# Image tokenizer's synthesis split by column bands, GpSimd's rotation in three functions, and new written orders of a step for all engines

## What is computed

```python
def reference(x, cls_tok, ...):
    h = tok(x)            # rec = idwt2(rec, h * w[0], v * w[1], d * w[2]), level by level
    h = concatenate([cls_tok, h], axis=1)
    h = h + attn(layernorm(h))
    h = h + ffn(layernorm(h))
```

## Time and profile before

| | |
|---|---|
| median of 3 runs | 1755.23 us (1753.16 to 1758.5) |
| span of the profiled execution | 1750.5 us, first to last instruction; no other time of that execution is given |
| PE busy | 1664.2 us, 95% |
| DVE busy | 1470.0 us, 84% |
| ACT busy | 1323.6 us, 76% |
| POOL busy | 1120.1 us, 64% |

### The profile page before, as it was taken

One profiled execution on the slowest core, in us unless ns is written; L12 is line 12 of the kernel. 1 busy time (PEld: TensorE's weight loads), 2 busy tenths in 40 slices (PEclk: granted clock), 3 DMA queues, 4 the chain that ended last, 5 costly groups with the idle time before them and its releaser, 6 DMA issues.

```text
span 1750.5 us, 48653 instructions
## 1 busy us (share of the span) xinstructions
PE 1664.2 (95%) x16742; PEld 1278.3 (73%) x16742; DVE 1470.0 (84%) x4972; ACT 1323.6 (76%) x3812; POOL 1120.1 (64%) x1034
## 2 busy tenths in 40 slices
PE   7758999999999999999999999999999999999975
PEld 6635777777777777777777777777777777777653
DVE  3837888899888888899888888899888888889874
ACT  0326888888888888888888888888888888888762
POOL 0087667766777666766777667666677667666500
PEclk9789999999999999999999999999999999999986
DMA  9311111111111111111111111111111111111100
GB/s 320 110 61 61 56 53 56 53 67 57 61 68 68 59 61 57 50 65 62 56 68 68 66 55 60 54 56 66 55 64 68 68 53 61 56 53 62 44 7 13
DMA packets 90168, 113.70 MB, mean 65 GB/s; under 512 B 14818, under 2 KB 52163, under 8 KB 89667
## 3 DMA queue, kind: packets, MB, share of 16 engines
q1 hardware_dynamic: 89922, 110.59, 18.1%
HBM read 26.62 MB, written 8.42 MB: 20 GB/s over the span
## 4 chain that ended last, share of the span: by engine, by line
PE 88%; DVE 4%; SPq 3%; POOL 2%; ACT 1%; issue 1%; DMA 0%; DVEq 0%; POOLq 0%; ACTq 0%
PE bank L725 45%; PE bank L842 9%; PE bank L983 7%; PE bank L831 6%; PE bank L829 6%; PE bank L994 3%; PE bank L853 3%; PE bank L903 3%; PE bank L891 2%; PE bank L1003 2%; SPq L320 1%; PE bank L882 1%; DVE arena L1283 1%; PE bank L950 0%; POOL rot L486 0%
## 5 line engine op out<-in xcount | busy, mean ns | idle before, releaser
L482 POOL TENSOR_TENSOR arena<-rq,cos 128x512 f32<-128x512 f32 x256 | 326.1, 1274 | 280.0 <-ACT rq L526 280.0
L535 ACT ACTIVATE arena<-arena,nm 128x129 f32<-128x129 f32 (+1 forms) x1024 | 455.6, 455 | 0.0
L486 POOL TENSOR_TENSOR rot<-rot,sin 128x512 f32<-128x512 f32 x256 | 326.3, 1275 | 103.9 <-DMA rot<-rq 103.9
L725 PE MATMUL bank<-xt_h,weights 128*128 128x256 f16 x2048 | 378.9, 273 | 9.2 <-ACT rq L526 7.8
L526 ACT ACTIVATE rq<-bank,bqk 128x256 f32<-128x256 f32 x512 | 214.4, 471 | 170.1 <-PE bank L725 155.3
L1283 DVE CUSTOM_DVE_ANT_0 arena<-bank,bias 128x129 f32<-128x129 f32 (+1 forms) x1024 | 317.9, 352 | 26.5 <-issue 16.6
L489 POOL TENSOR_TENSOR arena<-arena,rot 128x512 f32<-128x512 f32 x256 | 314.2, 1228 | 37.3 <-POOL rot L486 0.9
L1291 DVE TENSOR_TENSOR ptr_l<-bank,ptr_h 128x384 f16<-128x384 f32 x512 | 280.0, 552 | 31.8 <-ACT ptr_h L545 29.4
L545 ACT ACTIVATE ptr_h<-bank 128x384 f16<-128x384 f32 x512 | 249.1, 486 | 68.6 <-PE bank L725 44.0
L725 PE MATMUL bank<-xt_l,weights 128*128 128x256 f16 x1024 | 279.6, 273 | 0.0
L842 PE MATMUL bank<-eye,arena 128*128 128x128 f32 x1536 | 253.0, 277 | 8.5 <-DVE ptr_l L1291 4.4
(11 more groups left out here) (200 smaller groups left out, 3182.5 us busy)
## 6 DMA issues: line engine op xcount, KB each, us to landing
rot<-rq SPq DMA_DIRECT2D x512, 128.0 KB, 2.0
arena<-in_x SPq DMA_DIRECT2D x4, 2048.0 KB, 15.2
xin<-in_x SPq DMA_DIRECT2D x32, 256.0 KB, 2.8
hr<-hr SPq DMA_DIRECT2D x32, 256.0 KB, 2.3
out<-h SPq DMA_DIRECT2D x64, 128.0 KB, 2.1
arena<-in_L_attn_w_qkv SPq DMA_DIRECT2D x2, 1536.0 KB, 8.6
weights<-in_L_ffn_w_down SPq DMA_DIRECT2D x1, 1024.0 KB, 11.8
arena<-in_L_ffn_w_gate SPq DMA_DIRECT2D x1, 1024.0 KB, 8.5
```

Of the source, the lines that this page charges most:

```text
L482: pool.tensor_tensor(dst, rq[:, g % 2].rearrange("p j (t n) -> p j t n", t=T), cos[:, :].rearrange("p (t n) -> p t n", t=T).unsqueeze(1).b ...
L486: pool.tensor_tensor(r, r, sin[:, :].unsqueeze(1).broadcast_to([P, 2, SIDE]), ALU.mult).then_inc(t2_ready, 1)
L535: act.activation(cols, cols, ACT.Exp, bias=nm[:, t, h:h + 1], scale=-1.0, accum_out=rs[:, t, h:h + 1]).then_inc(e_done, 1)
L725: ins = pe.matmul(dst, lhs[l], rhs[r], start=start and n == 0, stop=stop and n == len(parts) - 1)
```

## The change

It changes how tokens are made. POOL now takes sums and differences of neighbouring columns, level by level (`column_bands`), into a tile `haar` of 512 columns: 256, 128, 64 and 64 for the four column bands. `synthesise` multiplies each by its row operator, four matmuls of these widths into `b_bank`; `coarse` is gone. ACT copies the bank to `syn` (`synthesis_out`), and POOL undoes the column transform in six instructions (`image_back`) that write `hh`; DVE's `image_out` is gone. The gates' coefficients are set up for this in the first part, with four terms in place of three. `project(b, 5)` waits for ACT's copy in place of `hh`. `rotate` on POOL becomes `cosine`, `sine` and `turned_sum`, which stand apart in the order. Epsilon is added to the two variances by two instructions of one column each. Each engine's step has a new order, SP's too: there `store(s - 2, 1)` now stands ahead of `rotate(s, 0)`, and the load of an image waits for POOL's first column step, not for PE's product.

```diff
-BANDS, OPS, TERMS, BLOCK = 10, 4, 3, 8
+BANDS, OPS, TERMS, BLOCK = 10, 4, 4, 8
...
-                sp.wait_ge(syn_ready, a)
+                sp.wait_ge(coeffs, 3 * a - 2)
                 load_x(a)
...
             def step(s):
                 rotate(s - 1, 3)
                 rotate(s - 1, 4)
-                load(s + 1)
                 rotate(s - 1, 5)
+                rotate(s - 1, 7)
                 rotate(s - 1, 6)
-                rotate(s - 1, 7)
-                store(s - 3, 1)
+                move(s - 2)
+                store(s - 2, 0)
+                load(s + 2)
+                store(s - 2, 1)
                 rotate(s, 0)
                 rotate(s, 1)
                 rotate(s, 2)
-                move(s)
-                store(s - 2, 0)
...
+
+                pool.tensor_tensor(high, src[:, :, 0::2], src[:, :, 1::2], ALU.subtract)
+                return pool.tensor_tensor(low, src[:, :, 0::2], src[:, :, 1::2], ALU.add)
+
+            def column_bands(first):
+
+                d1, d2, d3, low = columns(haar)
+                column_step(s1[:, :, :], d1, xin).then_inc(coeffs, 1)
+                pool.wait_ge(coeffs, first)
+                column_step(s2[:, :, :], d2, s1).then_inc(coeffs, 1)
+                pool.wait_ge(coeffs, first + 1)
+                column_step(low, d3, s2)
+
             def first_operators():
 
...
-                pool.tensor_tensor(rowop[:, :, :].rearrange("p o (b r) -> p o b r", r=BLOCK),
-                                   ops[:, 0, :, :].unsqueeze(2).broadcast_to([P, OPS, P // BLOCK, BLOCK]),
-                                   avg[:, 2, :].rearrange("p (b r) -> p b r", r=BLOCK).unsqueeze(1).broadcast_to([P, OPS, P // BLOCK, BLOCK]), ALU.mult).then_inc(rowop_ready, 1)
+                build_rowop(ops[:, 0, :, :])
...
 
             def row_operators(a):
                 if not image(a) or a == 0:
                     return
                 pool.wait_ge(ops_ready, 2 if a <= 16 else 3)
                 pool.wait_ge(syn_ready, a)
-                pool.wait_ge(coarse_ready, a)
                 pool.tensor_copy(op_now[:, :, :], ops[:, bass.ds(a, 1), :, :].rearrange("p a o r -> p (a o) r")).then_inc(coeffs, 1)
                 pool.wait_ge(x_in, 16 * (a + 1))
-                pool.tensor_tensor(s1[:, :, :], xin[:, :, 0::2], xin[:, :, 1::2], ALU.add).then_inc(coeffs, 1)
-                pool.wait_ge(coeffs, 3 * a + 2)
-                pool.tensor_tensor(rowop[:, :, :].rearrange("p o (b r) -> p o b r", r=BLOCK),
-                                   op_now[:, :, :].unsqueeze(2).broadcast_to([P, OPS, P // BLOCK, BLOCK]),
-                                   avg[:, 2, :].rearrange("p (b r) -> p b r", r=BLOCK).unsqueeze(1).broadcast_to([P, OPS, P // BLOCK, BLOCK]), ALU.mult)
-                pool.tensor_tensor(s2[:, :, :], s1[:, :, 0::2], s1[:, :, 1::2], ALU.add).then_inc(coeffs, 1)
-                pool.wait_ge(coeffs, 3 * a + 3)
-                pool.tensor_tensor(s3[:, :, :], s2[:, :, 0::2], s2[:, :, 1::2], ALU.add).then_inc(rowop_ready, 1)
+                column_bands(3 * a + 1)
+                build_rowop(op_now[:, :, :])
+
+            def image_back(a):
+                if not image(a) or begun and a == 0:
+                    return
+                d1, d2, d3, low = columns(syn)
+                pool.wait_ge(syn_out_done, a + 1)
+                pool.tensor_tensor(quad_sum[:, :, 0::2], low, d3, ALU.add)
+                pool.tensor_tensor(quad_sum[:, :, 1::2], low, d3, ALU.subtract).then_inc(back, 1)
+                pool.wait_ge(back, 2 * a + 1)
+                pool.tensor_tensor(pair_sum[:, :, 0::2], quad_sum[:, :, :], d2, ALU.add)
+                pool.tensor_tensor(pair_sum[:, :, 1::2], quad_sum[:, :, :], d2, ALU.subtract).then_inc(back, 1)
+                pool.wait_ge(back, 2 * a + 2)
+                if a:
+                    pool.wait_ge(hr_ready, a)
+                    pool.wait_ge(xn_ready, a)
+                pool.tensor_tensor(hh[:, :, 0::2], pair_sum[:, :, :], d1, ALU.add)
+                pool.tensor_tensor(hh[:, :, 1::2], pair_sum[:, :, :], d1, ALU.subtract).then_inc(h_ready, 1)
...
-            def rotate(b, g):
+            def cosine(b, g):
                 if not image(b):
...
+                pool.tensor_tensor(rope_out(b % 2, GROUPS[g]), rq[:, g % 2].rearrange("p j (t n) -> p j t n", t=T),
                                    cos[:, :].rearrange("p (t n) -> p t n", t=T).unsqueeze(1).broadcast_to([P, 2, T, P]), ALU.mult).then_inc(pcos_done, 1)
+
+            def sine(b, g):
+                if not image(b):
+                    return
                 pool.wait_ge(rot_done[g % 2], 128 * b + 32 * (g // 2 + 1))
                 r = rot[:, g % 2]
                 pool.tensor_tensor(r, r, sin[:, :].unsqueeze(1).broadcast_to([P, 2, SIDE]), ALU.mult).then_inc(t2_ready, 1)
+
+            def turned_sum(b, g):
+                if not image(b):
+                    return
+                dst = rope_out(b % 2, GROUPS[g])
                 wait_cos(pool, b, g)
                 pool.wait_ge(t2_ready, 8 * b + g + 1)
-                pool.tensor_tensor(dst, dst, r.rearrange("p j (t n) -> p j t n", t=T), ALU.add).then_inc(qk_done, 1)
+                pool.tensor_tensor(dst, dst, rot[:, g % 2].rearrange("p j (t n) -> p j t n", t=T), ALU.add).then_inc(qk_done, 1)
 
...
             first_operators()
+            image_back(0)
+            begun = True
             pool.wait_ge(late_in, 16 * 13)
 
             def step(s):
-                rotate(s + 1, 0)
-                rotate(s + 1, 1)
-                rotate(s + 1, 2)
-                row_operators(s + 2)
+                cosine(s + 1, 0)
+                add_bias(s + 1)
+                sine(s + 1, 0)
+                cosine(s + 1, 1)
+                turned_sum(s + 1, 0)
+                sine(s + 1, 1)
+                cosine(s + 1, 2)
+                turned_sum(s + 1, 1)
                 token_rstd(s)
-                rotate(s + 1, 3)
-                rotate(s + 1, 4)
-                rotate(s + 1, 5)
+                sine(s + 1, 2)
+                cosine(s + 1, 3)
+                turned_sum(s + 1, 2)
+                sine(s + 1, 3)
+                image_back(s + 2)
+                turned_sum(s + 1, 3)
+                cosine(s + 1, 4)
                 image_rstd(s + 2)
-                rotate(s + 1, 6)
-                rotate(s + 1, 7)
-                add_bias(s + 2)
+                cosine(s + 1, 5)
+                sine(s + 1, 4)
+                sine(s + 1, 5)
+                turned_sum(s + 1, 4)
+                turned_sum(s + 1, 5)
+                cosine(s + 1, 6)
+                cosine(s + 1, 7)
+                sine(s + 1, 6)
+                row_operators(s + 3)
+                turned_sum(s + 1, 6)
+                sine(s + 1, 7)
+                turned_sum(s + 1, 7)
...
 
-            def coarse_out(a):
+            def synthesis_out(a):
                 if not image(a):
                     return
-                act.wait_ge(coarse_ready, a + 1)
+                act.wait_ge(syn_ready, a + 1)
                 if a:
                     act.wait_ge(h_ready, a)
-                act.activation(pair_sum[:, :, :].rearrange("p t n -> p (t n)"), u_bank[:, 0:SIDE], ACT.Copy).then_inc(coarse_out_done, 1)
+                act.activation(syn[:, :], b_bank[:, :], ACT.Copy).then_inc(syn_out_done, 1)
...
-                pe.matmul(b_bank[:, :], rowop[:, 0, :], xin[:, :, :].rearrange("p t n -> p (t n)"), start=True, stop=True).then_inc(syn_ready, 1)
-
-            def coarse(a):
...
-                    if o > 0:
-                        rhs = rhs.unsqueeze(2).broadcast_to([P, T * n, 128 // n])
-                    ins = pe.matmul(u_bank[:, 0:SIDE], rowop[:, o + 1, :], rhs, start=o == 0, stop=o == 2)
-                ins.then_inc(coarse_ready, 1)
+                for o, (dst, src) in enumerate(zip(columns(b_bank), columns(haar))):
+                    ins = pe.matmul(dst.rearrange("p t n -> p (t n)"), rowop[:, o, :], src.rearrange("p t n -> p (t n)"), start=True, stop=True)
+                ins.then_inc(syn_ready, 1)
 
             def project(b, g):
                 if not image(b) or begun and (b, g) == (0, 0):
@@ -911,7 +958,7 @@
                 if g == 0:
                     pe.wait_ge(xtl_done, b + 1)
                 elif g == BEFORE_SYN and image(b + 1):
-                    pe.wait_ge(h_ready, b + 2)
+                    pe.wait_ge(syn_out_done, b + 2)
                 else:
                     pe.wait_ge(rq_ready, 8 * b + g)
                 for i in range(2):
...
-                ts(shifted[:, :], agg[:, :, 1], 1e-5, None, ALU.add).then_inc(ready, 1)
+                for t in range(T):
+                    ins = ts(shifted[:, t:t + 1], agg[:, t, 1:2], 1e-5, None, ALU.add)
+                ins.then_inc(ready, 1)
...
-                if not image(a) or begun and a == 0:
-                    return
-                dve.wait_ge(syn_ready, a + 1)
-                dve.wait_ge(coarse_out_done, a + 1)
...
```

(24 more changed lines are left out.)

348 lines of the change are left out of this document (160 added, 188 removed).

## The result

The changed kernel takes 1806.67 us (median of 4 runs, 1805.67 to 1810.37), the kernel before 1754.66 beside it: a ratio of 1.0307, 95% interval 1.0289 to 1.0325. The forecast was 1754 us with a range of 1712 to 1770. It was wrong.

A forecast was written before the change was run, and what follows sets the result against it. PE was taken as the bound at 49.04 us per step; -1.3 of product and +1.6 of wait gave +9 us, the ends -8, so 1756 by the sum, stated as 1754 us, range 1712 to 1770.

The forecast's parts named there:

- The place and the mechanism of the wait: PE at project_v(s, 1) waits for DVE's values_lo(.., 0), delayed by normalise_image blocked by POOL: 1.6 us per step.
- The size of the block: DVE's two normalise_image instructions, held up by POOL's unbroken run: +1.3 us per step (0.9 to 1.6).
- PE's product: Synthesis on PE: 2.26 us go, 0.96 come, so PE's work falls 1.3 us per step (1.07 to 1.39).
- The step that failed: PE's step: nothing behind project_v(s, 1) makes its wait good, so 49.3 us per step, +9 us over 29 steps.
- rival 1: No wait on POOL, or DVE has time: step 47.7 plus 0 to 0.3, 1709 to 1718 us; 0.32 with halfway cases.
- Rival 2: SP's store ahead of rotate(s, 0) makes POOL's chain late and DVE wait at image_stats: 1783 us; chance 0.15.
- The first part: Start, images 0 and 1: PE's 6.54 us wait for s3 shrinks as row_operators(1) moves ahead; -8 us (-13 to -3).
- The end: Last 84 us, holding no synthesis, with the chain that of the last block: 0 us (-2 to +3).

The follow-up runs named there:

- e1: Changed kernel with normalise_image written as scalar_tensor_tensor, rstd broadcast along the row, instead of tensor_scalar, same place in every order; 1794.97 us.
- e6: Changed kernel with xn of images 1 to 31 as an accumulating tensor_scalar in the same place, leaving out the factor rstd; 1759.82 us.
- e10: Changed kernel with SP's store(s-2,1) moved behind rotate(s,2) instead of ahead of rotate(s,0); 1806.03 us.
- e8: Kernel before the change with normalise_image(s-1) moved ahead of reciprocals(s-3,2) on DVE; 1826.57 us.
- e9: e8 with xn of images 1 to 31 as an accumulating tensor_scalar, leaving out the factor rstd; 1782.19 us.
- e14: Changed kernel with accumulating xn (no rstd, images 1 to 31), DVE's image_stats behind gate_up(s-3,0), POOL's image_rstd behind sine(s+1,5); 1789.08 us.
- e15: Changed kernel with xn (images 1 to 31) on ACT behind values_hi(s+1,0), image_stats behind gate_up(s-3,0), image_rstd behind sine(s+1,5); 1771.69 us.

## Why the prediction was wrong, step by step

- **The place and the mechanism of the wait**: right. `project_v(s, 1)` waits for `values_lo(., 0)`, because the pair of `xn` now meets POOL's rotations. Forecast 1.6 us per step; the mean is 1.36. What the prediction takes from the Trainium skill (SBUF — State Buffer, Who interferes with whom) on the tensor_scalar agrees with the 2.24 us of the earlier trace rows and the 2.39 here. The same section says that an instruction with two inputs in SBUF contends with a GpSimd instruction that reads SBUF, and that the tensor_scalar that writes out an accumulator does not enter the modes that contend. The 1069 and the 474 ns of e1 and e6 agree with both.
- **The size of the block**: too small. "The second by a whole one, 1.27 less what it would overlap: +1.3 us (0.9 to 1.6)" is +1.74 in the mean (2.39 less 0.65), and +2.04 in the step shown. The two instructions were held up by 0.8 and 0.9 us in the mean, not by 0.6 and what is left of 1.27. This is 0.4 us per step in the mean.
- **That the wait came out near its forecast** is luck in part. In the step shown, DVE's stretch from the start of `residual` to the end of `values_lo(., 0)` is 22.2 us where the forecast has 21.2 (19.91 and 1.3), and PE's from the end of `attention_out` is 20.9 (22.58 less the 1.65 idle) where it has 19.9. Both are too short by 1.0, and the difference hides it.
- **PE's product**: 1.3 us forecast, bounds 1.07 to 1.39. By the starts, 2.26 less 1.05 is 1.21. Three of the four narrow passes take 0.11 us, as one of 128 columns does, and the first takes 0.06; the weight loads in front of them, of 128 columns, start 0.11 apart. The row of 64-column loads that I called nearest was not. The Trainium skill (TensorE: Matmul & The Clock Gate, LDWEIGHTS) gives a load as its columns divided by 1.2, in ns; the estimate from it for 128 columns, 107 ns, agrees with these 0.11. Worth 3 us in all.
- **The step that failed**: "the wait at `project_v(s, 1)` becomes 1.6 us. Nothing behind it makes it good [...]: 49.04 - 1.3 + 1.6 = 49.3 us per step." This sum holds only if PE waits nowhere else in the new order. It does, and for reasons that have nothing to do with the block: e6, with the block gone and no wait at `project_v(., 1)`, has a step of 49.41, where the prediction's rival 1 gave 47.7 to 48.0. 1.5 us per step went there: 0.39 at `gate_up(., 1)`, 0.30 at `values(., 15)`, and the rest in pieces of at most 0.2. I had followed DVE against PE to one meeting point and taken the rest of a wholly new list to be as tight as the old one.
- **Rival 1** (no block, 1709 to 1718): wrong by the same 1.5 us. Without the block it would have been 1760. So the saving of PE's product would have been lost anyway.
- **Rival 2** (SP's store makes POOL late, 1783): not so. e10 moves the store and the time stays.
- **The first part**: -8 forecast; from the product of image 0 to that of image 2 it is -3.0. PE's two waits for `s3` there, 10.9 us with the 6.54 of the earlier trace rows, are gone. But its waits for ACT's `rq` grew from 8.9 to 14.5 us, those for `xn` from 2.3 to 4.0, and one of 2.9 for DVE's `gs` is new. The longest of those for `rq` in the changed kernel:

```profile
108.33 0.28 PE L783 MATMUL bank<-xt_h,weights 128*128 128x256 f16 x1 [2.11 <-ACT rq L584]
112.00 0.28 PE L783 MATMUL bank<-xt_h,weights 128*128 128x256 f16 x1 [2.19 <-ACT rq L584]
115.92 1.31 PE L950 MATMUL bank<-haar,rowop 128*128 128x256 f32 x8 [2.44 <-ACT rq L584]
...
127.03 0.28 PE L783 MATMUL bank<-xt_h,weights 128*128 128x256 f16 x1 [3.94 <-ACT rq L584]
```

  The first product comes 6.6 us later in the profiled execution. The kernels e8 and e9, whose start has the text of the kernel before, have it at 74.4 and 78.8 us. DVE waits 12.5 us for the load of `in_L_ffn_w_up` in e8 and 13.4 in the kernel before, but 18.8 in e9 and 19.6 in the changed kernel; so most of the 6.6 us goes with that load and not with the change.
- **The end**: 0 (-2 to +3) forecast, -3.0 measured, counted from the last product.

The sum with the measured terms: 1750.5 + 54.7 + 6.6 - 3.0 - 3.0 = 1805.8.

Shown by experiments: the block costs 47 of the 52 us, in the changed kernel and likewise put into the kernel before. Shown too: the new product's shorter time came out in neither order, old or new, in any of the kernels that move DVE's, ACT's or POOL's work around it. Argued from these and not shown: that in both orders DVE's row from `residual` to `turn_input` is what holds the step at 49.4 to 49.7 us once the block is gone. e14 speaks for it, and e15 against it as the only cause. An order in which it does come out may exist; I did not find one.

## What to carry to other kernels

Where a list for all engines is new, one meeting point is not enough. Follow the engine that is serial to each point at which PE waits for it, up to the next place where that engine is idle, and give a forecast of "the rest stays as it was" a range of its own: here it was 1.5 us per step. Work that looks idle may be what fills another engine's delay, as `coarse` did for ACT and `image_stats` for DVE; taking it out or moving it gives back less than its length. And an elementwise instruction on DVE in a form that POOL holds up belongs where POOL is idle, or in a form that it does not hold up.

## What the runs showed of the hardware

- `scalar_tensor_tensor` with both inputs in SBUF (128x256, f32) is held up by POOL as `tensor_scalar` is: in e1 the mean is 1069 ns (window 588 to 980) against 473 for the shortest. The accumulating `tensor_scalar` in the same place took 469 to 480 ns in all 62 cases of e6, with POOL running.
- The `tensor_scalar` of one column that adds epsilon was not held up: it took 143 to 156 ns in all 130 cases of the changed kernel. The one of two columns in the kernel before (L1328) took 168 to 1256 ns in 65 cases.
- A pass of 64 columns in f32 takes 0.11 us on PE from start to start, a pass of 128 columns 0.109, with other weights of 128 columns loaded for each; only the first of the four narrow passes, behind the passes of 128 columns, takes 0.06.
- POOL writing every second column takes longer than reading every second one: 0.73 and 0.46 us for 256 and 128 columns against 0.615 and 0.401. The six of the way back took 3.0 us in place of the 2.6 that I had summed. From the changed kernel's timeline of POOL:

```profile
878.65 0.33 POOL L480 TENSOR_TENSOR quad_sum<-syn 128x64 f32<-128x64 f32 x1
879.07 0.46 POOL L482 TENSOR_TENSOR pair_sum<-quad_sum,syn 128x128 f32<-128x128 f32 x1
...
880.03 0.73 POOL L488 TENSOR_TENSOR hh<-pair_sum,syn 128x256 f32<-128x256 f32 x1
```
